# A new order of the two pairs' stages on PE, ACT, DVE and Pool, and a DMA of its own for the first expert's gates

## The reference

```python
h = jax.nn.gelu(jnp.einsum('end,edh->enh', xe, W1) + b1[:, None, :], approximate=False)
y = jnp.einsum('enh,ehd->end', h, W2) + b2[:, None, :]
sel = jnp.take_along_axis(jnp.transpose(y, (1, 0, 2)), top_idx[:, :, None], axis=1)
out = (weights[:, :, None] * sel).sum(axis=1)
```

## Time and profile before

| | |
|---|---|
| median of 3 runs | 269.35 us |
| the profiled execution's own time | 269.56 us |
| its span, first to last instruction | 267.5 us |
| mean granted TensorE clock | 0.942 |
| PE busy | 231.0 us, 1206 matmuls |
| DVE busy | 149.3 us, 266 instructions |
| ACT busy | 129.5 us, 206 instructions |
| POOL busy | 45.1 us, 44 instructions |

### The profile page before, as it was taken

How to read it: one execution, slowest core, us unless ns; L and a number is a source line. 1 busy time by engine, 2 the same in 40 slices (tenths; PEclk the granted TensorE clock), 3 DMA queues, 4 the chain that set the end, 5 groups by cost and what they waited for, 6 DMA issues and landing times.

```text
span 267.5 us, 3160 instructions
## 1 busy us (share of the span) xinstructions
PE 231.0 (86%) x1206; PEld 121.8 (46%) x1206; DVE 149.3 (56%) x266; ACT 129.5 (48%) x206; POOL 45.1 (17%) x44
## 2 busy tenths in 40 slices
PE   3487689999985698969439999999999999999994
PEld 3385479757442477759324223222223333333331
DVE  0691939999696990676887324432443334433344
ACT  2147641021720707043637567556655676666760
POOL 3750077003770008202120000000000000000000
PEclk9869999999997959997957999999999999999999
DMA  7990000000000000000005907043150705043001
GB/s 235 209 208 8 2 0 4 0 0 2 0 0 0 1 0 2 0 0 0 2 1 143 192 1 157 0 108 91 49 108 2 194 2 142 16 104 96 0 0 39
DMA packets 6430, 14.18 MB, mean 53 GB/s; under 512 B 2704, under 2 KB 4112, under 8 KB 5392
## 3 DMA queue, kind: packets, MB, share of 16 engines
q1 hardware_dynamic: 6416, 13.99, 22.3%
HBM read 12.81 MB, written 1.18 MB: 52 GB/s over the span
## 4 chain that ended last, share of the span: by engine, by line
PE 72%; DVE 13%; ACT 8%; DMA 3%; issue 1%; SPq 1%; DVEq 0%; ACTq 0%
PE psum L611 22%; PE psum L626 22%; DMA xs<-in_x 3%; PE psum L524 3%; PE psum L470 3%; PE psum L442 3%; PE psum L452 3%; PE psum L540 2%; PE psum L478 2%; PE psum L487 2%; ACT place L661 2%; PE psum L383 1%; PE psum L558 1%; ACT place L722 1%; DVE place L957 1%; PE psum L433 1%
## 5 line engine op out<-in xcount | busy, mean ns | idle before, releaser
L768 ACT ACTIVATE hid<-psum,b1p 128x512 f32<-128x512 f32 x128 | 77.7, 688 | 41.3 <-PE psum L611 41.3
L611 PE MATMUL psum<-tok,w1s 128*128 128x512 f16 x256 | 64.4, 388 | 0.1
L1061 DVE SCALAR_TENSOR_TENSOR term<-psum,sm,wide 128x512 f32<-128x512 f32 x32 | 24.0, 751 | 70.8 <-PE psum L626 68.0
L626 PE MATMUL psum<-hid,w 128*64 128x512 f32 x256 | 61.8, 604 | 0.0
L611 PEld LDWEIGHTS psum<-tok,w1s 128*128 128x128 f16 x256 | 21.7, 99 | 51.3 <-ACT hid L768 28.0
L626 PEld LDWEIGHTS psum<-hid,w 128*64 128x64 f32 x256 | 15.6, 136 | 32.1 <-issue 26.3
L1066 DVE TENSOR_TENSOR x<-x,term 128x512 f32<-128x512 f32 x32 | 22.1, 692 | 1.1
L470 PE MATMUL psum<-h_pad,tap_bd 128*128 128x512 f32 x36 | 15.8, 592 | 0.0
L383 PE MATMUL psum<-c,xs 128*128 128x128 f32 x32 | 7.3, 423 | 8.3 <-DMA xs<-in_x 8.3
L895 DVE SCALAR_TENSOR_TENSOR place<-h_pad,sm,place 128x512 f32<-128x512 f32 x16 | 12.0, 752 | 0.6
L524 PE MATMUL psum<-place,wide 128*128 128x64 f32 x64 | 9.8, 327 | 2.7 <-DVE wide L964 2.7
(11 more groups left out here) (135 smaller groups left out, 306.0 us busy)
## 6 DMA issues: line engine op xcount, KB each, us to landing
wide<-gate_store SPq DMA_DIRECT2D x16, 512.0 KB, 6.4
xs<-in_x SPq DMA_DIRECT2D x2, 512.0 KB, 6.3
w1f<-in_W SPq DMA_DIRECT2D x2, 512.0 KB, 12.7
block_out<-x SPq DMA_DIRECT2D x4, 256.0 KB, 6.4
hid<-in_W1T SPq DMA_DIRECT2D x1, 512.0 KB, 12.2
w<-in_W SPq DMA_DIRECT2D x1, 512.0 KB, 14.8
c<-const SPq DMA_DIRECT2D x1, 483.5 KB, 4.0
sm<-in_small SPq DMA_DIRECT2D x1, 407.0 KB, 6.3
```

The lines of the kernel that those rows point to most:

```text
L611: mm = pe.matmul(h_bank(n), w1s[:, part, e, k * P:(k + 1) * P], tok[:, pair, half, b, :], start=part == 0, stop=part == 1)
L626: mm = pe.matmul(y_bank(u)[b * H:(b + 1) * H, :], w2[:, e * KT + k, :], hid[:, u % 2, B2 * k + b, :], start=k == 0, stop=k == KT - 1)
L768: act.activation(hid[:, u % 2, t, :], h_bank(n), ACT.Gelu, bias=b1p[:, e * KT + k:e * KT + k + 1]).then_inc(gelu_ready, 1)
L1061: dve.scalar_tensor_tensor(term[:, u % 2, :], y_bank(u), b2t[:, e:e + 1], gate_b[part][:, e % (E // 2), :], ALU.add, ALU.mult).then_inc(te ...
```

## The change

Three things are changed. `TURN` gets new numbers, `unit_turn` a new formula, so that the order of the stages changes on PE, ACT and DVE. On POOL the order that the new numbers give is the same as before. And the first load of buffer 0 is cut in two: the gates of the first expert (two DMAs of 128 KB, with a semaphore of their own) and those of the other three (two of 384 KB). L1061 of unit 0 waits for the first, that of unit 1 for the second.

```diff
--- before.py
+++ after.py
@@ -41,19 +41,20 @@
 
 
 TURN = {
-    "weights_of_first": (0, 0), "dct_over_h": (0, 2), "square_columns": (1, 3), "dct_over_w": (4, 9), "windows": (5, 12), "conv_in": (6, 20),
-    "keep_dw": (7, 11), "keep_xd": (8, 14), "gelu_in": (10, 16), "norm_columns": (13, 17), "places": (15, 21),
-    "keep_xt": (18, 25), "join": (19, 38), "high": (22, 79), "gram_matrices": (23, 26), "gram_times_w": (24, 30),
-    "first_taps": (27, 35), "norms": (28, 41), "mask_gram": (29, 34), "second_taps": (31, 50), "logits": (32, 52),
-    "products": (33, 36), "keep_tk": (37, 45), "inverse_norms": (39, 46), "scale_logits": (39.7, 46.1), "norms_of_k": (40, 55),
-    "softmax_in": (42, 61), "gelu_second": (43, 57), "softmax_out": (44, 74), "gelu_depthwise": (47, 53),
-    "gelu_out": (48, 68), "conv_out": (49, 63), "project": (51, 65), "exponent": (54, 66), "heads": (56, 69),
-    "times_wv": (58, 72), "keep_y": (59, 70), "low": (60, 73), "mask_mix": (62, 81), "keep_yt": (64, 76),
-    "to_frequencies": (67, 85), "inverse_over_kh": (71, 90), "keep_back": (75, 82), "keep_half": (77, 86),
-    "square_tokens": (78, 92), "mix_branches": (80, 83), "inverse_over_kw": (84, 91), "high_part": (87, 100),
-    "tokens": (88, 94), "residual": (89, 96), "norm_tokens": (93, 97), "keep_tokens": (95, 110), "features": (98, 103),
-    "low_part": (99, 106), "router": (101, 113), "route": (104, 111), "gates_to_rows": (112, 118),
-    "shares": (107, 116), "biases": (39.5, 39.5), "tanh_gap": (109, 115), "keep_gates": (112, 119),
+    "weights_of_first": (1, 1), "dct_over_h": (1, 2), "square_columns": (1, 2), "dct_over_w": (3, 6),
+    "windows": (4, 8), "conv_in": (5, 9), "keep_dw": (3, 6), "keep_xd": (4, 7), "gelu_in": (5, 9),
+    "norm_columns": (1, 2), "places": (7, 10), "keep_xt": (8, 10), "join": (2, 4), "high": (3, 5),
+    "gram_matrices": (11, 12), "gram_times_w": (13, 14), "first_taps": (3, 7), "norms": (15, 19), "mask_gram": (4, 5),
+    "second_taps": (16, 21), "logits": (17, 22), "products": (6, 8), "keep_tk": (11, 13), "inverse_norms": (9, 14),
+    "scale_logits": (11, 15), "norms_of_k": (18, 26), "softmax_in": (12, 17), "gelu_second": (12, 20),
+    "softmax_out": (13, 18), "gelu_depthwise": (14, 18), "gelu_out": (15, 22), "conv_out": (20, 27),
+    "project": (23, 29), "exponent": (16, 21), "heads": (24, 30), "times_wv": (25, 31), "keep_y": (17, 23),
+    "low": (28, 33), "mask_mix": (16, 20), "keep_yt": (19, 24), "to_frequencies": (32, 37),
+    "inverse_over_kh": (34, 38), "keep_back": (25, 28), "keep_half": (26, 29), "square_tokens": (27, 31),
+    "mix_branches": (19, 21), "inverse_over_kw": (35, 39), "high_part": (30, 33), "tokens": (36, 40),
+    "residual": (22, 24), "norm_tokens": (23, 25), "keep_tokens": (32, 34), "features": (41, 43), "low_part": (6, 7),
+    "router": (42, 44), "route": (26, 28), "gates_to_rows": (45, 141), "shares": (27, 111), "biases": (10, 10),
+    "tanh_gap": (35, 101), "keep_gates": (36, 141),
 }
 
 UNITS = STEPS * E
@@ -61,7 +62,7 @@
 
 def unit_turn(u):
 
-    return {-1: 114, 0: 117}.get(u, 119 + u)
+    return 100 + 10 * (u + 1)
 
 
 def in_turn(stages, experts=None):
@@ -314,6 +315,7 @@
 
         w1_done, gelu_ready, w2_done, term_done, add_done, gates_out = (
             sem(n) for n in "w1_done gelu_ready w2_done term_done add_done gates_out".split())
+        first_gate_in = sem("first_gate_in")
         gate_in = [sem(f"gate_in{n}") for n in range(2)]
 
         block = ctx.enter_context(nc.Block())
@@ -347,10 +349,20 @@
                 pair, half = divmod(i, 2)
                 if n > 1:
                     sp.wait_ge(term_done, (E // 2) * (n - 1))
-                for b in range(B2):
-                    rows = gate_store[pair, half, b:b + 1, part * E // 2 * CHUNK:(part + 1) * E // 2 * CHUNK]
-                    sp.dma_start(gate_b[part][b * H:(b + 1) * H].rearrange("p e n -> p (e n)"),
-                                 rows.broadcast_to([H, E // 2 * CHUNK])).then_inc(gate_in[part], 16)
+                first, last = part * E // 2, (part + 1) * E // 2
+
+                def load(e0, e1, signal):
+
+                    for b in range(B2):
+                        rows = gate_store[pair, half, b:b + 1, e0 * CHUNK:e1 * CHUNK]
+                        sp.dma_start(gate_b[part][b * H:(b + 1) * H, e0 - first:e1 - first, :].rearrange("p e n -> p (e n)"),
+                                     rows.broadcast_to([H, (e1 - e0) * CHUNK])).then_inc(signal, 16)
+
+                if n == 0:
+                    load(first, first + 1, first_gate_in)
+                    load(first + 1, last, gate_in[part])
+                else:
+                    load(first, last, gate_in[part])
 
             def store_out(i):
 
@@ -1054,7 +1066,9 @@
                 x1p = bank(x1[:, pair, :], half)
                 dve.wait_ge(w2_done, u + 1)
                 part = e // (E // 2)
-                if e % (E // 2) == 0:
+                if u == 0:
+                    dve.wait_ge(first_gate_in, 16 * B2)
+                elif u == 1 or e % (E // 2) == 0:
                     dve.wait_ge(gate_in[part], 16 * B2 * (i + 1))
                 if u > 1:
                     dve.wait_ge(add_done, u - 1)
```

## The result

The changed kernel takes 259.91 us (median of 4 runs, 258.73 to 262.81), the kernel before beside it 269.0 us. The ratio is 0.9656, 95% interval 0.9601 to 0.9711: 3.4% faster, 9.3 us. The forecast was 262.5. The profiled execution took 260.44 us in all with a span of 258.4, 9.1 us less than before. Ratios here leave out runs that lie over 1.5% above the fastest of the same kernel; where that matters the single runs are given.

The account below looks back on a forecast made before the run. PE's two expert lines (122.4 us) bound the kernel unchanged; only the start of up(0) can move. Order -9.0, gates -0.1, clock +2.25 give -6.85: 262.7 against 269.56, or 262.5 against the median; range 257 to 267.5.

Parts of the forecast that it names:

- Step 1: Front, 27 to 51 us: earlier POOL release holds first_taps0; second_taps0 at 51.2 (+0.2 to +0.3), free bound 50.2.
- Step 2: Up to 77 us: order on PE, DVE and ACT as before but for small swaps; softmax_out0 ends at 76.65, +0.2.
- Step 3: join1 no longer holds inverse_norms1, about 1.8 us goes; k norms at 81.2 instead of 82.9.
- Step 4: mask_mix0 ahead of softmax_in1, the main part: mask_mix0 starts 83.2, low0 ends 91.6 instead of 97.87, softmax_in1 starts 86.0.
- Step 5: high1 on POOL holds both L973 of mix_branches0, 3.3 us given back; low1 101.65 to 105.45, ending at 113.2 before.
- Step 6: Both pairs' inverse transforms and tokens: tokens1 ends at 119.8 instead of 127.93, -8.1.
- Step 7: Tail: up(0) follows gates_to_rows0 after 0.3 instead of 1.17 us, -0.9; up(0) starts at 132.3, -9.0 in all.
- Step 8: First gate load: uncut it would cost 1.0 us in the new order; with the cut -0.1, bounds -0.4 to +1.5.
- Step 9: PE's clock falls only in the 2.1 us pause before to_frequencies0; low1 takes 6.04, +2.25, bounds 0 and +5.5.
- A: Rival: no fall of PE's clock at 100 us, 260.3 us; chance 0.18.
- B: Rival: neither clock fall nor hold, L895 and L973 run free on DVE, 257.0 us; chance 0.12.
- C: Rival: clock falls in all three pauses, or softmax_in1 comes later by as much, 265.7 us; chance 0.24.

Follow-up runs that it names:

- e1: The changed kernel run again, nothing altered, with a second profile; 0.9622 of the kernel before, six runs from 257.99 to 263.13 us.
- e4: The changed kernel with POOL's three W1 instructions released earlier, by the first half of keep_xd1 instead of keep_xt0; 0.986 of the kernel before, 265.23 us.
- e5: The changed kernel with mask_mix0 put behind softmax_in1 on DVE again; 0.9853 of the kernel before, runs of 263.69, 266.55 and 267.48 us.
- e6: The changed kernel with ACT's old order restored: gelu_depthwise1 ahead of exponent0, gelu_second1 ahead of keep_y0; 0.9672 of the kernel before, 260.03 to 261.68 us.
- e8: The kernel before with one swap alone, mask_mix0 ahead of softmax_in1 on DVE; 1.0173 of the kernel before, 273.05 to 275.32 us.
- e7: The changed kernel with high1 on POOL held back until mix_branches0 is done; 0.960 of the kernel before, from two runs at 257.98 and 260.19 us.
- e10: The changed kernel with keep_tokens1 behind tanh_gap0 on ACT and gates_to_rows0 ahead of router1 on PE again; 0.9683 of the kernel before.
- e2: The changed kernel with the single first gate load put back, new order kept; 0.9723 of the kernel before, median 261.42 us.
- e3: The kernel before with only the cut of the first gate load, old order kept; 1.0014 of the kernel before.
- e9: The changed kernel with pair 1's norm and routing moved behind the first expert units, up(0) ahead of gates_to_rows0; 0.956 of the kernel before, median 258.7 us.
- e11: As e9, with router1 one unit later and route1, tanh_gap1, shares1, gates_to_rows1, keep_gates1 also later; 0.9448 of the kernel before, median of six 258.41 us.

## Why the prediction was right, step by step

- **The bound.** Right. The expert phase kept its length, and `up(0)` starting earlier is the whole gain.
- **Step 1** was wrong in its place, right in its mechanism. I put POOL's release at 31.7, with two taps left; it came at 32.38 with the last tap under way, and `second_taps0` started at 50.18, my free bound, not at 51.2. In this execution DVE's `first_taps0` ran 0.35 us earlier than in the trace of before and `keep_xt0` 0.5 us later than I had it, since PE had the low clock in `conv_in0` (L422, 3.78 us for 1.98) and behind it. In e1 the release came at 31.58 and a tap took 3.98 us, as I had said, and still `second_taps0` started at 49.37. So the hold is real (e1, e4), but with one tap caught (e1) or two (e5) it costs nothing, since PE has both gram matrices to do in that time. The cost that I gave this step was wrong, and so was the sum of its free bound: from the first gram matmul, at 35.58 and not 35.0, to `second_taps0` PE took 14.6 us and not 4.0 + 11.2. That 50.2 came out is a coincidence.
- **Step 2** kept its order, but as step 1 cost nothing, `second_taps1` and all around it came 0.9 us before the walk.
- **Step 3** happened (L876 0.23 us); by e6 beside e1 it is worth 0.8 us, not the 1.8 us of the hold, since a pause before `times_wv0` comes in its place.
- **Step 4** was right: L976 at 82.99 for 83.2, `low0` ending at 91.86 for 91.6, `softmax_in1` at 86.73 for 86.0. e5 gives the swap 5.5 us, a part of them through the clock and the hold of L969, which the step did not have. e8 shows that it needs more of the new order; which part is not shown.
- **Step 5** was right: both L985 held, 2.49 and 2.46 us, `low1` 101.67 to 105.46 for 101.65 to 105.45. e7 adds what I had not seen: without the hold, `high1` itself would be late.
- **Step 6**: `tokens1` ended at 119.47 for 119.8. **Step 7**: `up(0)` at 131.93 for 132.3, and 0.90 us by e10.
- **Step 8** was right on both sides: the cut protects 0.8 us (1.0 predicted, e2, by the profiles) and gives nothing in the old order (e3).
- **Step 9 failed.** It said that the clock falls in the pause at 100 us and costs 2.25 us. It didn't, in this profile or in those of e1, e2, e4 and e9 to e11 (`low1` 3.79 to 3.80 us): the pause was 1.15 us instead of 2.1, because `times_wv1` ended at 99.38 and not at 98.3 (0.7 of it from `softmax_out1`, 94.14 for 93.45), and `low1` took 3.79. It fell at 81 instead, after 1.26 us, where I had said that it would not, and cost 1.6 us in L527. And e1 shows the same pause without a fall. Two errors nearly cancelled, the 1 us that step 1 didn't cost and the 1.6 us of this fall, so that the times agree from `mask_mix0` on. The sum without step 9's 2.25 is 260.5; the profiled execution took 260.44.
- **Luck.** That agreement to a tenth is luck. In e1, where no group from `second_taps0` to `tokens1` ran at the lower clock, as in my walk, `mask_mix0` started at 81.45 for 83.2, `tokens1` ended at 117.02 for 119.8 and `up(0)` started at 129.48 for 132.3. The walk was 2.8 us too long there, 1.8 of them by `second_taps0`. The forecast of 262.5 lies 2.6 us above the median of the first four runs and 1.1 above that of e1's six, and 2.25 us of it stand for a fall that did not come.

The rival that came true is A by its number and by its condition, no fall at 100 us; that the clock fell elsewhere is not in it. B's free L985 and C's three falls did not happen, and D's low clock through the stage did not either.

## What to carry to other kernels

Where engines run written-out orders, walk the new order stage by stage from durations of the old trace: here 130 us of it came out within half a microsecond at most places in one execution, with two errors cancelling, and 2.8 us too long in another. What it can't give is the clock, so leave the clock as a spread on both sides and don't put one fall into the sum; and read in the old trace how much of its time is low clock behind a pause, since an order with shorter pauses may win that too (by my estimate 4.8 of 9.3 us here). Before a move on ACT or PE that releases a GpSimd instruction earlier, look what VectorE does at that moment: in e4 each of three GpSimd instructions of 2 to 4 us held one of VectorE's with two SBUF inputs, and a change of one wait cost 8.4 us on VectorE and 6.5 us of the kernel. Holds count only where something waits for the held engine: one or two held taps cost the kernel nothing (e1, e5). And ask of each wait that is to be removed who waits for the waiting engine: the cut of the gate load is worth nothing in one order and 0.8 us in the other.

## What the runs showed of the hardware that was not expected

- The same pause, two clocks: nine profiles of the new order and its variants have a pause of 1.24 to 1.26 us before the first `times_wv`. In four of them the clock had fallen (3.58, 3.54, 3.41 and 3.39 us: the changed kernel, e5, e7, e11), in five it had not (1.99 to 2.07 us: e1, e2, e4, e9, e10). The same goes for the pause of 1.64 us before `conv_in0`: it took 1.98 us in the profile of before and 3.49 us in that of e2. The runs of the changed kernel range from 257.99 to 263.13 us, with mean granted clocks from 0.973 down to 0.948.
- POOL and DVE took turns in e4: one L907 stands between L851 and L852 and one between L852 and L853 (the three held L907 take 3.98, 2.3 and 4.44 us), and POOL's instructions grow as well, L852 from 1.89 to 2.23 us.
- One execution of e8 took 779.62 us (span 777.6) and one of the kernel before 576.58, both with a granted clock of 1.0 in the records. The first was profiled. DVE's and POOL's busy times in it are near those of before (146.4 and 44.6 us), ACT's is 141.7 against 129.5, and PE's is 758.7 us for the same 1206 matmuls, against 231.0.

```profile
L611 PE MATMUL psum<-tok,w1s 128*128 128x512 f16 x256 | 212.6, 1079 | 0.0
L626 PE MATMUL psum<-hid,w 128*64 128x512 f32 x256 | 212.2, 1869 | 0.0
```

A matmul of L611 takes 1079 ns there, against 388 in the profile of before. What slowed TensorE is not shown by anything in the trace.
